# Moving the first tap of the convolutions to GpSimd and placing the preparation work anew in a selective-scan kernel

## What is computed

```python
for i in range(8):                                   # layers
    xin, z = split(x @ W_in.T)                       # 512 inner channels each
    xin = silu(sum(up[:, k:k + L, :] * w[:, k] for k in range(4)) + b)   # causal conv, 4 taps
    dt, Bm, Cm = split(xin @ W_x.T)
    delta = softplus(dt @ W_dt.T + bdt)
    # for each of 16 states n:
    #   h = h * exp(delta * A[n]) + (delta * xin) * Bm[n];   y += h * Cm[n]
    x = x + ((y + xin * Dp) * silu(z)) @ W_out.T
```

## Time and profile before

| | us |
|---|---|
| median of 3 runs | 7742.98 (7742.54 to 7743.24) |
| the profiled execution | 7743.71 |
| its span, first to last instruction | 7742.0 |
| VectorE busy | 6668.0 (86%) |
| ScalarE busy | 6422.9 (83%) |
| TensorE busy | 6941.3 (90%) |
| GpSimd busy | 5929.2 (77%) |

### The profile page before, as it was taken

The page is one execution under the profiler, slowest core; times in us unless marked ns, Lnnn a source line. Parts: engine busy times, 40 slices in busy tenths (PEclk is TensorE's granted clock), DMA queues, the critical chain, the costliest instruction groups (busy, mean ns, idle before and its releaser), DMA issues. The chain is left out here.

```text
span 7742.0 us, 143629 instructions
## 1 busy us (share of the span) xinstructions
PE 6941.3 (90%) x39999; PEld 4801.8 (62%) x39999; DVE 6668.0 (86%) x6510; ACT 6422.9 (83%) x10314; POOL 5929.2 (77%) x4917
## 2 busy tenths in 40 slices
PE   6979999999999999999999999999999999999997
PEld 4646666666666666666666666666666666666665
DVE  3259988988998899889889988988998898889888
ACT  1258888888888888888888888888888888888887
POOL 2148887888888888888888887888888788888875
PEclk9989999999999999999999999999999999999998
DMA  4111111111111111111111111111111111111112
GB/s 161 34 42 40 40 39 47 43 39 40 42 45 44 39 39 48 42 40 39 40 46 44 40 38 41 45 42 39 39 48 42 39 40 41 45 43 39 40 39 91
DMA packets 222613, 352.40 MB, mean 46 GB/s; under 512 B 43856, under 2 KB 78448, under 8 KB 221712
## 3 DMA queue, kind: packets, MB, share of 16 engines
q1 hardware_dynamic: 218048, 332.70, 14.6%
q0 software_dynamic: 3792, 10.38, 0.4%
HBM read 325.00 MB, written 17.98 MB: 44 GB/s over the span
## 5 line engine op out<-in xcount | busy, mean ns | idle before, releaser
L884 POOL TENSOR_TENSOR drive<-du,brep 128x512 f32<-128x512 f32 x4096 | 5505.9, 1374 | 708.3 <-DVE du L1127 385.6
L916 ACT ACTIVATE ps_d<-delta,cur 128x512 f32<-128x512 f32 x4096 | 2869.9, 701 | 373.9 <-DVE state L1077 354.8
L923 ACT ACTIVATE prod<-ps_r,cT 128x512 f32<-128x512 f32 x4096 | 2837.1, 693 | 245.4 <-PE ps_r L1231 243.9
L1231 PE MATMUL ps_r<-ident,state 128*128 128x128 f32 x16384 | 2564.0, 280 | 297.1 <-ACT prod L923 158.3
L1077 DVE TENSOR_TENSOR_SCAN state<-ps_d,carry,drive 128x512 f32<-128x512 f32 x2048 | 2517.7, 1266 | 260.6 <-ACT ps_d L916 258.5
L1077 DVE TENSOR_TENSOR_SCAN state<-ps_d,drive 128x512 f32<-128x512 f32 x2048 | 2396.8, 1206 | 245.6 <-ACT ps_d L916 233.0
L1238 PE MATMUL ps_y<-ident,prod 128*128 128x128 f32 x16384 | 2481.9, 276 | 25.9 <-ACT prod L923 25.9
L1238 PEld LDWEIGHTS ps_y<-ident,prod 128*128 128x128 f32 x16384 | 1938.9, 142 | 666.8 <-issue 499.4
L1231 PEld LDWEIGHTS ps_r<-ident,state 128*128 128x128 f32 x16384 | 1851.3, 142 | 729.9 <-ACT prod L923 462.5
L1278 PE MATMUL ps_r<-xm,w_inz_sb 128*128 128x512 f32 x1024 | 507.4, 618 | 81.6 <-ACT prod L923 81.6
L1270 PE MATMUL ps_r<-xm,w_inx_sb 128*128 128x512 f32 x1024 | 509.1, 620 | 21.9 <-ACT prod L923 14.2
(11 more groups left out here) (144 smaller groups left out, 4647.3 us busy)
## 6 DMA issues: line engine op xcount, KB each, us to landing
brep<-bc_dram SPq DMA_DIRECT2D x1024, 256.0 KB, 3.2
w_sb<-w SPq DMA_DIRECT2D x8, 1024.0 KB
w_all<-w SPq DMA_DIRECT2D x8, 1024.0 KB, 11.4
xb<-xs_dram SPq DMA_DIRECT2D x39, 128.5 KB, 2.0
w_all<-x SPq DMA_DIRECT2D x4, 1024.0 KB, 9.1
w_inx_sb<-w_in SPq DMA_DIRECT2D x8, 512.0 KB, 4.1
w_inz_sb<-w_in SPq DMA_DIRECT2D x8, 512.0 KB, 4.5
w_out_sb<-w_out SPq DMA_DIRECT2D x8, 512.0 KB, 4.2
```

The costliest lines, as they stand in the source:

```text
L884: nc.gpsimd.tensor_tensor(drive[:, k % DRIVE, :], du[:, j, :], brep[:, n % BREP, :], ALU.mult).then_inc(drive_set, 1)
L916: nc.scalar.activation(ps_d[:, k % 2, :], delta[h][:, j, :], ACT.Exp, scale=cur[h][:, a:a + 1]).then_inc(decay_set, 1)
L923: nc.scalar.activation(prod[:, t, :], ps_r[:, item_place(U, h, kind, item), :], ACT.Copy, scale=cT[(h + 1) % 2 if item[1] == "prev" else h ...
L1231: last = nc.tensor.transpose(out[:, j * P:(j + 1) * P], state[STATE_IN[n]][:, j, t * P:(t + 1) * P], ident[:])
```

## The change

1. The first tap of blocks 0, 1 and 2 (`xc = xpad * tap + bias`) is issued by GpSimd (`conv` in its block) after the drive at places `TAP_AT` = (7,3), (12,2), (14,3). VectorE issues taps 1 to 3 as before, the first of them behind a wait for the new semaphore `conv_begun`. The waits for `xpad`, the taps and `u_set` move to GpSimd.
2. ScalarE's decays are issued by a table, `DECAYS`: one at each place, with one more at the seven places of `BOOST_AT` and one less at the seven of `REST_AT`.
3. All tables of places have new numbers.

```diff
-SILU_AT, EXP_AT, LN_AT = (4, 2), [(7, 0), (10, 1)], [(8, 3), (11, 3)]
-CONV_AT = [(5, 2), (5, 2), (6, 0), (6, 2), (9, 2), (10, 1), (12, 2), (12, 3), (15, 1), (17, 0), (17, 3), (19, 0)]
+SILU_AT = (4, 3)
+TAP_AT = [(7, 3), (12, 2), (14, 3)]
+BOOST_AT = [(1, 0), (1, 3), (5, 2), (5, 3), (6, 0), (12, 2), (15, 1)]
+REST_AT = [(0, 0), (2, 2), (3, 0), (3, 3), (7, 3), (8, 2), (14, 0)]
+LEAD = 2
...
+DECAYS, at = {}, LEAD
+for n, j in [(n, j) for n in range(STATES) for j in range(CB)]:
+    count = 1 + BOOST_AT.count((n, j)) - REST_AT.count((n, j))
+    DECAYS[n, j] = list(range(at, at + count))
+    at += count
...
+            def conv(copied, G, h, j):
+
+                wait_counted(ring_act, copied)
+                if j == DVE_CONV[0]:
+                    wait_counted(taps_in[h], loads_of(G, h))
+                    if not is_first(G):
+                        wait_counted(u_set, G)
+                nc.gpsimd.tensor_scalar(xc[:, j, :], xpad[:, j, TAPS - 1:TAPS - 1 + T], taps[h][:, j * TAPS + TAPS - 1:j * TAPS + TAPS],
+                                        taps[h][:, COL_CB + j:COL_CB + j + 1], ALU.mult, ALU.add).then_inc(conv_begun, 1)
...
-                        k = CB * n + t + 2
-                        if k < TILES:
-                            exponent(U, h, k)
-                        elif kind != "last":
-                            exponent(U + 1, 1 - h, k - TILES)
+                        for k in DECAYS[n, t]:
+                            if k < TILES:
+                                exponent(U, h, k)
+                            elif kind != "last":
+                                exponent(U + 1, 1 - h, k - TILES)
...
-                if k == 0:
-                    dve.wait_ge(ring_act, copied)
...
+                if k == 1:
+                    dve.wait_ge(conv_begun, CV * G + DVE_CONV.index(j) + 1)
```

More of the change, by code:

```diff
@@ L870, in keep_carry, with early, late @@
                 nc.gpsimd.tensor_copy(carry[:, n, :], state[STATE_IN[n]][:, :, T - 1]).then_inc(carried, 1)
+            def conv(copied, G, h, j):
[6 more added lines that the diff above has]
+                                        taps[h][:, COL_CB + j:COL_CB + j + 1], ALU.mult, ALU.add).then_inc(conv_begun, 1)
+            def early(U, h, kind, G, it, n, j):
+                for i in range(CV):
+                    if (n, j) == TAP_AT[i]:
+                        conv(item_read(U, kind, f"X{DVE_CONV[i]}"), G, h, DVE_CONV[i])
+            def late(copied, F, hf, n, j):
+                for i in range(CV):
+                    if (n + STATES, j) == TAP_AT[i]:
+                        conv(copied, F, hf, DVE_CONV[i])
             def unit(U, h, it, kind):
@@ L892, in unit @@
                                 halo(U, kind, F, hf)
+                            late(items_before(U, kind)[2], F, hf, n, j)
                         if kind in ("first", "mid"):
@@ L899, in _ @@
             mask_x(0, "pre0", 0, 0, 0)
+            for i in range(CV):
+                conv(item_read(0, "pre0", f"X{DVE_CONV[i]}"), 0, 0, DVE_CONV[i])
             halo(0, "pre1", 0, 0)
             mask_x(0, "pre1", 1, 1, 0)
+            for n in range(STATES):
+                for j in range(CB):
+                    for i in range(CV):
+                        if (n, j) == TAP_AT[i]:
+                            conv(item_read(0, "pre1", f"X{DVE_CONV[i]}"), 1, 1, DVE_CONV[i])
             units(pool, unit)
@@ L1051, in _ @@
                     early(0, 0, "pre1", 1, n, t)
-            exponent(0, 0, 0)
-            exponent(0, 0, 1)
+            for k in range(LEAD):
+                exponent(0, 0, k)
             units(act, unit)
@@ L1102, in keep_alive, with conv @@
                                              alive[0][:, T - 1:T] if hf == 1 else 1.0, ALU.add, ALU.max).then_inc(ring_vec, 1)
-            def conv(copied, G, h, j, k):
+            def conv(G, h, j, k):
                 tap = TAPS - 1 - k
                 w = taps[h][:, j * TAPS + tap:j * TAPS + tap + 1]
-                if k == 0:
-                    dve.wait_ge(ring_act, copied)
[L1110 to L1115, removed]
-                else:
-                    dve.wait_ge(conv_step, (TAPS - 1) * (CV * G + DVE_CONV.index(j)) + k)
-                    step = nc.vector.scalar_tensor_tensor(xc[:, j, :], xpad[:, j, tap:tap + T], w, xc[:, j, :], ALU.mult, ALU.add)
+                if k == 1:
+                    dve.wait_ge(conv_begun, CV * G + DVE_CONV.index(j) + 1)
+                else:
+                    dve.wait_ge(conv_step, (TAPS - 2) * (CV * G + DVE_CONV.index(j)) + k - 1)
+                step = nc.vector.scalar_tensor_tensor(xc[:, j, :], xpad[:, j, tap:tap + T], w, xc[:, j, :], ALU.mult, ALU.add)
                 step.then_inc(conv_done if k == TAPS - 1 else conv_step, 1)
@@ L1194, in unit @@
                         if kind != "last":
-                            late(items_before(U, kind)[2], U + 1, 1 - h, n, j)
+                            late(U + 1, 1 - h, n, j)
                         if kind in ("first", "mid"):
@@ L1207, in _ @@
                 for j in range(CB):
-                    late(items_before(0, "pre1")[2], 0, 0, n, j)
+                    late(0, 0, n, j)
                     early(0, 1, "pre1", 1, 0, n, j)
```

41 lines of the change are left out of this document (24 added, 17 removed).

## The result

| | before | changed |
|---|---|---|
| median, us | 7743.1 (7742.5 to 7744.6) | 7674.1 (7666.7 to 7684.1) |
| ratio | | 0.9911, 95% interval 0.9894 to 0.9929 |
| the profiled execution | 7743.7 | 7684.1 |
| its span | 7742.0 | 7682.3 |
| VectorE busy | 6668.0 | 6700.2 |

The account below looks back on a forecast made before the run. ScalarE was taken to set the pace behind the SiLUs, VectorE for the rest. Per unit 4.0 + 1.25 - 0.6 - 0.2 = 4.5 us, over 64 units 288 us, from 7743 to 7455 us; range 7330 to 7615.

Parts of the forecast that it names:

- Part 2: First taps leaving VectorE: those of blocks 1 and 2 give 1.25 us per unit, bounds 0.9 to 1.8.
- Part 1: Stretch behind the SiLUs, decay 19 to scan 38: gain of 4.0 us per unit, bounds 2.0 to 5.4.
- ScalarE's walk: ScalarE's steps added up from decay 19's end: decay 30 at 21.8, scan 38 at 36.3, with 0.5 added 36.8.
- The signs given for the waits: VectorE's waits for decays down from 491.5 to about 360 us, those for `xpad` gone, hardly any for GpSimd.
- Part 3: Rest of the unit, places 34 to 52: 0.6 us per unit lost, bounds 0.3 to 1.5.
- Part 4: First taps on GpSimd at 1.0 us each: 0.2 us per unit lost, bounds 0 to 1.5.
- the wait for X2: Tap 2 on GpSimd, behind drive 59, waits for X2, which ScalarE reads at place 56, ending 3.4 after scan 55.
- (a): Postponed weighings cost decays at places 31 to 56, giving back half of part 1: 7583 us, chance 0.14.
- (d): New order only moves VectorE's holes; parts 1 and 3 cancel, GpSimd eats the taps' 1.25: 7743 us, chance 0.07.
- (c): GpSimd, with taps of 4.6 us each, becomes the bound and VectorE waits for it: 7890 us, chance 0.07.

Follow-up runs that it names:

- before_skip: The kernel before with the first taps and the bias left out, the second tap adding the shifted input: 7709.1 us (0.9948).
- short drives: The kernel before and the changed kernel, each with GpSimd drives of 256 instead of 512 columns, the other half staying zero: 7627.9 and 7484.5 us.
- after_onein: The changed kernel with GpSimd drives of one input over all 512 columns, B left out: 7479.7 us (0.9659).

## Why the prediction missed

In the profiled executions the forecast was 189 us less busy and 99 us less idle. Measured was 32 more busy and 92 less idle. Of the 221 between, 191 are longer durations of other instructions, all but some 15 of them held time. The last 30 are lost overlap: a scan that follows another at once begins 0.08 us before the record of the first ends, and where a decay comes only just in time it doesn't.

**Part 2 failed, and the sum with it.** It took the recorded durations of the taps that leave as gained, and those of all that stay as fixed. A first tap is 0.52 us of work. The 1.20 at 3046.26 was 0.52 and 0.68 of holding by a drive, and the mean of 985 in the earlier trace rows is nearly half holding. Undisturbed, two taps per unit are 1.05 us, or 0.9 less their overlaps, which is the lower bound and 0.35 under the 1.25 taken; at 22 us of 221 that is not the miss. The miss is the unwritten term "the other 93 instructions take what they took", which is 191/64 = 3.0 us per unit. `before_skip` shows the same at the old places, where the taps that leave give 34 us, 0.5 per unit, and the others grow by 105. It was in reach: the shortest tap of 0.72 stood beside a mean of 880 in the kernel before, and the earlier trace rows had the same instruction at two lengths.

**Part 1** had the right mechanism and was too large: 4.0 forecast, 2.8 measured (41.1 to 38.3 on average over the units). ScalarE's walk was good, decay 30 ends at 22.0 where 21.8 was worked out. Scan 38 began at 37.8 (h 0) and 38.9 (h 1), not 36.8 and 37.5. With short drives it came at 37.0 and 36.8, so the walk was right for a VectorE that nobody holds. And the reference contained holding: with short drives the kernel before has 39.8, not 41.1. The signs given for the waits did not agree with the sum either: 131 us less for decays and 93 less for `xpad` are 224, where the sum holds 99 of idle time. Measured were 61 and 93, less 42 more for GpSimd.

**Part 3** was forecast at 0.6 lost, with ScalarE's longer step at 0.35 of it. Scans 38 to 44 do step by 1.20 (h 0) and 1.18 (h 1). In the pair with short drives, where little is held, the lost overlap is 52 us, 0.8 per unit. If all of it belongs to this part, which no run separates, the term was too small, within its bounds. It explains, with the 72 us by which the first taps are shorter there (189.2 against 117.6), why that pair gains 143 and not 288: 288 - 72 - 52 = 164; of the other 21 us, 17 are steps that take longer even there and 4 idle time.

**Part 4** was right in the price of a tap and in the wait for X2. The taps on GpSimd take 0.78 where 1.0 was taken. Tap 2 waits as described:

```profile
L893 POOL TENSOR_SCALAR xc<-xpad,taps x192: 760/776/1675, 459.5 to 7410.1; 128x512 f32<-128x512 f32 x192
...
3054.33 0.77 POOL L893 TENSOR_SCALAR xc<-xpad,taps 128x512 f32<-128x512 f32 x1 [4.78 <-ACT xpad L974]
```

VectorE's waits for GpSimd rose by 42 us, 0.7 per unit where 0.2 was taken, in the bounds. What part 4 didn't price is what one more instruction on GpSimd does to VectorE without any semaphore: the taps there cost 40 us in all.

**The rivals.** The time lies between (a), 7583, and (d), 7743, nearer to (d), and came about by the mechanism of neither: the idle time that had left did not come back, and VectorE's waits for GpSimd took only 42 us of the gain. (c) had the right engine and the wrong path: GpSimd slows VectorE though it is hardly waited for. The signs that I had named for a wrong part 4, waits of scans for GpSimd over 1 us per unit, stayed below that mark (0.8) while the longer durations cost 3.0 per unit. The rule of the Trainium skill that I weighed, on GpSimd's speed, did not matter; the one on the shared ports did, and I left it out.

## What to carry to other kernels

Before counting an instruction's mean duration as a gain, set it against the shortest of its kind. The excess belongs to what runs beside it, and the next instruction pays it when this one leaves. After a change compare busy and idle time of the bounding engine apart; a step that has moved can cost in either, and time saved in one comes back in the other where a second engine is close behind. Where GpSimd multiplies in a stream beside VectorE's two-input steps, every entry of an order table also shifts who meets whom. Such an entry can't be priced from its own work, so try its neighbours.

## What the runs showed of the hardware

- A tap of two SBUF inputs that is held by GpSimd multiplications ends 0.55 us after the end of the one beside which it began, or of a later one: taps 0.72 alone, 4.47 at most in the changed kernel. TENSOR_SCALAR steps of one input are held too. The first taps of the kernel before (f32, 0.51 alone, 2.27 at most) end 0.28 after. `mark`'s second half (bf16) takes 0.66 alone and had a mean of 1.21. A tap held by one multiplication takes its own time and what was left of the multiplication, less 0.17 us; 69 taps of the changed kernel that began in the last 0.22 us of a drive were not held.
- It goes both ways. GpSimd's carry copy of 128x4 usually takes 0.19 us. Beside a softplus step of VectorE it takes 1.00, and ends within 0.05 of that step's end:

```profile
3021.30 1.20 DVE L1179 TENSOR_TENSOR low<-soft,low 128x1024 f32<-128x1024 f32 x1
```

```profile
3021.55 1.00 POOL L884 COPY carry<-state 128x4 f32<-128x4 f32 x1 [3.38 <-DVE state L1122]
```

- Scans with one input in PSUM are untouched: 1248 to 1287 ns over 2048 of them.
- A GpSimd instruction of one input holds VectorE's two-input steps as well: in `after_onein` all 32 taps held beside a drive end 0.53 to 0.55 us after a GpSimd instruction's end.
- On GpSimd one input costs much less than two: a 128x512 tap 0.76 us, a drive from one input 0.67 on average, against 1.25 for the multiplication of two.
